# First cross-attention on one Trainium2 core: every second score row passed over by VectorE in one 2048-column instruction, score banks in a cycle of four units

## The reference, cut to what matters

```python
q, k, v = _fq_sym(q, -1), _fq_sym(k, -1), _fq_sym(v, 2)   # round(x / s) * s, s = max|x| / 127
attn = jnp.einsum('bhqd,bhkd->bhqk', q, k)                 # 16 heads x 2048 queries x 2048 keys
attn = jax.nn.softmax(attn.astype(jnp.float32), axis=-1)
attn = _fq_unsigned(attn, axis=-1)                         # round(p / s) * s, s = max(p) / 255 of the row
out = jnp.einsum('bhqk,bhkd->bhqd', attn, v)
x = _layernorm(x + out @ Wp + bp)
```

## Time and profile before

| | |
|---|---|
| median of 3 runs | 2745.82 us (2744.62 to 2748.7) |
| the profiled execution | 2758.03 us, of which the trace's span is 2756.2 us |
| TensorE, matmuls busy | 2339.5 us (85%) |
| VectorE busy | 1871.3 us (68%) |
| ScalarE busy | 1590.1 us (58%) |
| GpSimd busy | 716.9 us (26%) |
| attention stage, first to last instruction of L1753 | 920.3 to 1589.0 us |

### The profile page before, as it was taken

How to read it: one execution, slowest core, us unless ns; L and a number is a source line. 1 busy time by engine, 2 the same in 40 slices (tenths; PEclk the granted TensorE clock), 3 DMA queues, 4 the chain that set the end, 5 groups by cost and what they waited for, 6 DMA issues and landing times. The chain is left out here.

```text
span 2756.2 us, 50448 instructions
## 1 busy us (share of the span) xinstructions
PE 2339.5 (85%) x16399; PEld 1534.9 (56%) x16545; DVE 1871.3 (68%) x4371; ACT 1590.1 (58%) x3099; POOL 716.9 (26%) x897
## 2 busy tenths in 40 slices
PE   6999999999987567777777779889997986899994
PEld 3676766767664334444444445545555664467773
DVE  5877778777774789999999912246665775234444
ACT  3656666566653579989999921056664654123332
POOL 1121121211211112222222200011111267436664
PEclk9999999999998799989889989989999998899997
DMA  5000000000001399999999930040000012446666
GB/s 198 1 1 0 0 0 0 0 0 0 0 0 46 65 207 183 176 185 180 179 184 183 186 77 1 0 148 1 1 1 7 13 64 78 143 86 110 108 108 143
DMA packets 539447, 211.18 MB, mean 77 GB/s; under 512 B 475002, under 2 KB 533878, under 8 KB 538230
## 3 DMA queue, kind: packets, MB, share of 16 engines
q1 hardware_dynamic: 518246, 180.54, 32.6%
q0 software_dynamic: 20592, 27.98, 5.9%
q10 hardware_dynamic: 416, 0.16, 0.0%
HBM read 54.27 MB, written 36.90 MB: 33 GB/s over the span
## 5 line engine op out<-in xcount | busy, mean ns | idle before, releaser
L1753 DVE TENSOR_SCALAR_CACHE_REDUCE x_row<-x_p_s,x_nsq 128x1024 f32<-128x1024 f32 x512 | 621.7, 1270 | 22.4 <-PE x_p_s L1528 22.3
L1632 ACT ACTIVATE x_ints<-x_row,x_nb 128x2048 uint16<-128x2048 f32 x256 | 511.5, 1999 | 46.4 <-DMA x_turned<-x_ints 27.6
L1528 PE MATMUL x_p_s<-x_kT,x_qz 128*128 128x512 bf16 x929 | 299.6, 412 | 145.0 <-DVE x_row L1753 137.6
L363 POOL TENSOR_TENSOR a_rstd<-a_ssq,neghalf 128x16 f32<-128x16 f32 x32 | 126.0, 3936 | 524.7 <-DVE a_ssq L874 524.7
L1528 PEld LDWEIGHTS x_p_s<-x_kT,x_qz 128*128 128x128 bf16 x1024 | 73.6, 101 | 266.7 <-DVE x_row L1753 238.7
L1656 POOL TENSOR_SCALAR x_nb<-x_low,x_hmin 128x1 f32<-128x1 f32 x256 | 75.0, 293 | 519.5 <-DVE x_row L1753 518.2
L3277 POOL DMA_INDIRECT f_acc<-f_yt,f_ids x111 | 171.9, 1548 | 136.3 <-ACT f_yt L3442 109.6
L1562 PEld LDWEIGHTS x_p_o<-x_vi,x_turned 128*128 128x128 f16 x4096 | 143.8, 98 | 87.1 <-DMA x_turned<-x_ints 18.7
L2216 ACT COPY s_eT<-sc_p_e 128x512 f32<-128x512 f32 x192 | 112.3, 585 | 133.7 <-PE sc_p_e L2106 133.6
L1562 PE MATMUL x_p_o<-x_vi,x_turned 128*128 128x16 bf16 x4096 | 143.0, 171 | 16.9 <-DMA x_turned<-x_ints 16.6
L3367 PE MATMUL f_p_g<-f_w,f_rowsT 128*128 x444 | 151.6, 464 | 0.0
(11 more groups left out here) (479 smaller groups left out, 5337.8 us busy)
## 6 DMA issues: line engine op xcount, KB each, us to landing
f_rows<-f_spread SPq DMA_DIRECT2D x111, 136.5 KB, 2.1
f_w<-in_L_ffn_w_dram SPq DMA_DIRECT2D x2, 2816.0 KB
x_turned<-x_ints SPq DMA_TRANSPOSE x224, 4.8
f_sum<-f_acc SPq DMA_DIRECT2D x6, 512.0 KB, 7.2
f_w<-in_L_ffn_w_dram SPq DMA_DIRECT2D x2, 1408.0 KB
f_spread<-f_empty SPq DMA_DIRECT2D x17, 136.5 KB, 2.6
x_res<-in_x_dram SPq DMA_DIRECT2D x2, 1024.0 KB, 6.9
a_wq<-in_L_attn_Wq_dram SPq DMA_DIRECT2D x2, 1024.0 KB, 11.0
```

Of the source, the lines that this page charges most:

```text
L363: pool.tensor_tensor(rstd[:, hs], ssq[:, hs], core.neghalf[:, 0:NH], ALU.pow).then_inc(root_h.sem, 1)
L1528: mm = pe.matmul(p_s[n % SLOTS][:, c * BANK:(c + 1) * BANK], qz[b % 2][:, par, a, :], kT[:, a, at:at + BANK], start=True, stop=True)
L1632: act.activation(ints[k][:, :], rows[k][:, :, :].rearrange("p s n -> p (s n)"), ACT.Exp, bias=nb[:, k:k + 1], scale=-1.0, accum_out=esum[: ...
L1753: dve.tensor_scalar(rows[k][:, half, :], p_s[n % SLOTS][:, :], nsq[:, b % 2, h:h + 1], HIGHEST, ALU.mult, ALU.min, accum_out=(low if half ...
```

## The change

The units with even `j` are passed over by one VectorE instruction of 2048 columns, which waits for all four matmuls and frees four banks at once. The odd units keep their two halves. The three slots become one tensor of six banks, and which pair of banks a half gets follows a cycle of four units (`PAIRS_OF`): an even unit gets two neighbouring pairs, (0, 1) or (1, 2), an odd one the pairs that come free around it. TensorE's order changes with it: at an odd step it makes the second half of that unit and both halves of the next one, at an even step only the first half of the next unit, and that behind `values`. `shift` uses `hmin` twice for an even unit, and `divided` moves from `j` = 4 to `j` = 5 on VectorE.

```diff
--- before.py
+++ after.py
@@ -1420,7 +1420,7 @@
         rden, o_raw, o, oT = sb("rden", [P, XH]), sb("o_raw", [P, H]), sb("o", [P, H]), sb("oT", [P, KT, P])
         y, stats, mv, ln_r = sb("y", [P, H]), sb("stats", [P, 6]), sb("mv", [P, 2]), sb("ln_r", [P, 1])
 
-        p_s = [ps(f"p_s{i}", [P, HALF]) for i in range(SLOTS)]
+        p_s = ps("p_s", [P, SLOTS * HALF])
         p_o, p_w = ps("p_o", [P, BANK]), ps("p_w", [P, BANK])
 
 
@@ -1437,6 +1437,20 @@
         v_turn, v_steps, v_scaled, v_up = (sem(n) for n in ("v_turn", "v_steps", "v_scaled", "v_up"))
         t_made, t_read = sem("t_made"), sem("t_read")
         block = ctx.enter_context(nc.Block())
+
+        PAIRS_OF = ((0, 1), (2, 0), (1, 2), (0, 2))
+        freed, last_user = {}, {}
+        for u in range(UNITS):
+            for half in range(2):
+                pair = PAIRS_OF[u % 4][half]
+                freed[u, half] = last_user.get(pair, 0)
+            for half in range(2):
+                last_user[PAIRS_OF[u % 4][half]] = 2 * u + (half + 1 if u % 2 else 2)
+
+        def scores_at(u, half, n=1):
+
+            at = PAIRS_OF[u % 4][half] * HALF
+            return p_s[:, at:at + n * HALF]
 
         def by_array(u):
 
@@ -1515,19 +1529,25 @@
                     mm = pe.matmul(p_w[:, 0:H], oT[:, t, :], wp[:, t, :], start=False, stop=(t == KT - 1))
                 mm.then_inc(y_made, 1)
 
-            def scores(u):
+            def scores(u, half):
                 b, j = divmod(u, PER_TILE)
                 a, par = divmod(j, 2)
                 if not j:
                     pe.wait_ge(qz_up, b + 1)
-                for half in range(2):
-                    n = 2 * u + half
-                    after(pe, half_up, n - SLOTS + 1)
-                    for c in range(2):
-                        at = half * HALF + c * BANK
-                        mm = pe.matmul(p_s[n % SLOTS][:, c * BANK:(c + 1) * BANK], qz[b % 2][:, par, a, :], kT[:, a, at:at + BANK],
-                                       start=True, stop=True)
-                    mm.then_inc(s_made, 1)
+                after(pe, half_up, freed[u, half])
+                for c in range(2):
+                    at = half * HALF + c * BANK
+                    mm = pe.matmul(scores_at(u, half)[:, c * BANK:(c + 1) * BANK], qz[b % 2][:, par, a, :], kT[:, a, at:at + BANK],
+                                   start=True, stop=True)
+                mm.then_inc(s_made, 1)
+
+            def scores_ahead(u):
+
+                if u % 2:
+                    scores(u, 1)
+                    if u + 1 < UNITS:
+                        for half in ((0, 1) if u % 4 == 1 else (1, 0)):
+                            scores(u + 1, half)
 
             def turn_ints(j, half):
                 def run(b):
@@ -1575,15 +1595,19 @@
                     mm = pe.matmul(p_o[:, t * P:(t + 1) * P], svcol[:, t, :], core.ident[:, :], start=True, stop=True)
                 mm.then_inc(v_turn, 1)
 
+            for half in range(2):
+                scores(0, half)
             for u in range(UNITS + PER_TILE):
                 if u < UNITS:
-                    scores(u)
+                    scores_ahead(u)
                 if not u:
                     turn_largest()
                 if u == 1:
                     turn_scales()
                 if 0 <= u - LATE < UNITS:
                     values(u - LATE)
+                if u < UNITS and not u % 2:
+                    scores(u + 1, 0)
                 jobs(u, {1: [(turn_x, 1)], 3: [(project_q, 1)], 5: [(turn_ints(2, 0), 0)], 6: [(turn_ints(2, 1), 0)],
                          7: [(turn_ints(4, 0), 0)], 8: [(turn_ints(4, 1), 0)],
                          10: [(turn_reps, 1)], 13: [(turn_o, -1)], 15: [(project_o, -1)]})
@@ -1653,7 +1677,8 @@
             def shift(u):
                 k = u % ROWS_KEPT
                 pool.wait_ge(half_up, 2 * u + 2)
-                pool.tensor_scalar(nb[:, k:k + 1], low[:, k:k + 1], hmin[:, k:k + 1], LOG_AMAX, ALU.min, ALU.add).then_inc(nb_up, 1)
+                other = low if u % 2 else hmin
+                pool.tensor_scalar(nb[:, k:k + 1], other[:, k:k + 1], hmin[:, k:k + 1], LOG_AMAX, ALU.min, ALU.add).then_inc(nb_up, 1)
 
             def heads(ap):
                 return ap.rearrange("p (h d) -> p h d", d=XD)
@@ -1744,13 +1769,19 @@
             def pass_over(u, half):
                 b, h = divmod(u, PER_TILE)
                 k = u % ROWS_KEPT
-                n = 2 * u + half
-                dve.wait_ge(s_made, n + 1)
+                whole = not u % 2
+                if whole and half:
+                    return
+                dve.wait_ge(s_made, 2 * u + (2 if whole else half + 1))
                 if not half:
                     after(dve, e_up, u - ROWS_KEPT + 1)
                     if not h:
                         dve.wait_ge(nsq_up, b + 1)
-                dve.tensor_scalar(rows[k][:, half, :], p_s[n % SLOTS][:, :], nsq[:, b % 2, h:h + 1], HIGHEST, ALU.mult, ALU.min,
+                if whole:
+                    dve.tensor_scalar(rows[k][:, :, :].rearrange("p s n -> p (s n)"), scores_at(u, 0, 2), nsq[:, b % 2, h:h + 1], HIGHEST,
+                                      ALU.mult, ALU.min, accum_out=hmin[:, k:k + 1]).then_inc(half_up, 2)
+                    return
+                dve.tensor_scalar(rows[k][:, half, :], scores_at(u, half), nsq[:, b % 2, h:h + 1], HIGHEST, ALU.mult, ALU.min,
                                   accum_out=(low if half else hmin)[:, k:k + 1]).then_inc(half_up, 1)
 
             def quantize_values():
@@ -1788,7 +1819,7 @@
                 jobs(u, {4: [(denominators, -1)], 5: [(inverse, 1)], 1: [(statistics, -2)]})
                 if u < UNITS:
                     pass_over(u, 1)
-                jobs(u, {3: [(largest, 1)], 4: [(divided, -1)], 1: [(moments, -2)]})
+                jobs(u, {3: [(largest, 1)], 5: [(divided, -1)], 1: [(moments, -2)]})
                 if u == ROWS_KEPT - 1:
                     quantize_values()
```

## The result

The changed kernel takes 2762.4 us (median of 3 runs, 2760.7 to 2763.8) against 2745.8: a measured ratio of 1.0044, 95% interval 1.0025 to 1.0064 (the two medians as they stand give 1.0060, inside it). It is slower, by 7 to 18 us, where 7.4 us less were forecast. The profiled execution took 2763.8 us.

The account below looks back on a forecast made before the run. VectorE was taken to bound the stage, with ScalarE close behind. The terms -17.4 + 3.5 + 5.5 + 1 = -7.4 us took 2745.8 to 2738.4 us; the forecast's own range was 2732 to 2743, the full range 2727 to 2757.

Parts of the forecast that it names:

- Costed at nothing: `project_q` and `turn_x` come one unit (2.4 us) later at ScalarE's queue; claimed hidden by four `rows` buffers, at no cost.
- at T + 2.3 against 2.4, no wait at the full clock: `divided`, moved behind the pass its `values` waits for; T is the end of the tile's last pass; no wait claimed.
- Term 1: VectorE's joined passes: 2.274 us for a whole pass, 0.136 saved on each of 128, -17.4 us (0 to 18.9 saved).
- Term 2: Bank fills freed only one half pass (1.20 us) ahead come late at the half clock: +3.5 us (0 to 7).
- Term 3: `project_o` before the next fill: at the half clock VectorE waits 1.6 us instead of 0.82, +5.5 us (0 to +18).
- Start and end: The first pass waits for four matmuls instead of two, and ScalarE is further behind at the end: +1 us.
- The long wait near 1000 us: VectorE's single 10.4 us wait for scores, where the next stage's weights are loaded; taken as unchanged.
- ScalarE becomes the bound: ScalarE's two waits are not absorbed, a tile costs 41.6 us instead of 40.82: +12.5, slower, 2758 us; chance 0.12.
- The clock gives way: TensorE at the half clock for twice the share, PEclk below about 0.85: +11, slower, 2757 us; chance 0.11.
- TensorE held by ScalarE: `turn_ints` waits in TensorE's queue for ScalarE's copy; about 8 us come through: 2746 us, no change; chance 0.20.
- Cover holds: The half clock falls elsewhere than on `project_o`, waits for scores stay as they are: 2729 us; chance 0.20.

Follow-up runs that it names:

- largest_late: The changed kernel with VectorE's `largest` and GpSimd's `scales` one unit later (`j` = 4 instead of 3): ratio 1.0008 to the kernel before.
- query_early: The changed kernel with `project_q` on TensorE one step earlier (`j` = 2 instead of 3): ratio 1.0001 to the kernel before, 1.0013 when measured again.
- before_query_late: The kernel before, without joined passes, with `project_q` on TensorE one step later (`j` = 4 instead of 3): ratio 1.0063 to the kernel before.
- split: The changed kernel with even units passed over by two 1024-column instructions again, banks and TensorE's order as changed: ratio 1.0122 to the kernel before.
- after_again: The changed kernel itself, measured once more beside the kernel before on another chip: ratio 1.0038 to the kernel before.

## Why the prediction was wrong

It gave 2738.4 us with a range to 2757.0; 2762.4 lies outside, on the slower side, which had a chance of 0.23.

- **The failed step: "Costed at nothing".** It saw that `project_q` and `turn_x` come one unit later, "and ScalarE's queue stands at both", and hid that behind the four `rows` buffers. ScalarE's queue was not the one that mattered. The copy `query_up` has another reader: `largest` on VectorE, at step 3 of the same tile. Measured: +20.2 us (21.4 against 1.2), in all 15 tiles. With it at zero or nearly so (`largest_late`, `query_early`) the kernel is level with before; with it alone (`before_query_late`) the kernel before loses 0.63%.
- **The same step, `divided`:** "at T + 2.3 against 2.4, no wait at the full clock". It waited 0.74 us right behind the timeline above (at 1242.10), 5.6 us up to 1605 us, where the kernel before has 0.5 beside the 7.1 of its last tile. At the full clock the margin held: `divided` did not wait in seven of the 15 tiles, and in all seven the granted clock was 1.00 in the stretch of the fills before it (3.4 to 0.6 us ahead). In seven others it waited 0.73 to 0.76 us, and there that clock was 0.50 (the last, at 0.73, waited 0.40). The prediction priced the half clock for two other places, and put it at nothing here.

```profile
1241.27 0.08 DVE L1784 DVE_READ_ACCUMULATOR x_row<-x_p_s,x_nsq 128x1 f32 x1
1242.10 0.42 DVE L1758 TENSOR_TENSOR x_o_raw<-x_p_o,x_rden 128x256 f32<-128x256 f32 x1 [0.74 <-issue]
```

- **Term 1, -17.4, was right but for 2 us.** A whole pass starts 2.27 to 2.28 us before the next (1236.44 to 1238.71, for one), where 2.274 was worked out. Added up over VectorE's timeline, from start to start without the waits, all passes but the last take 599.1 us against 614.6, so 15.5 are saved; the half passes take 1.209 each instead of 1.203. `split` confirms the sign.
- **Term 2, +3.5, in kind and size.** The whole pass of unit 14 waits 0.4 us in 12 of the tiles, 4.7 us in all; it lies within 0 to 7. In the 3 us before these waits the granted clock was 0.52 to 0.63, so they are the fills at the half clock that the term describes.
- **Term 3, +5.5, did not occur.** The kernel before has seven waits of 0.82 us behind `project_o` between 1040 and 1590 us (the prediction counted six); the change has none there. `project_o`'s weight loads, 1055 to 1600 us, last 190 ns from the shortest to the longest, which is the full clock, where the kernel before has a median of 264 over the stage. The chain holds at the full clock, as worked out. That I carried the share of half clock over, and placed it on this product, was the mistake: it stood at unit 14 and in front of `divided`. The rows of the two products (ns: shortest, median, longest), after:

```profile
L1529 PEld LDWEIGHTS x_p_w<-x_wp,x_oT x56: 190/190/190, 1062.0 to 1595.5; 128*128 128x128 f32 x56
```

and before:

```profile
L1515 PEld LDWEIGHTS x_p_w<-x_wp,x_oT x64: 190/264/337, 1017.5 to 1603.3; 128*128 128x128 f32 x64
```

- **Start and end, +1:** the tail alone took 2.9 us more, 1.6 of it by ScalarE's end. The long wait near 1000 us, taken as unchanged, went from 10.4 to 6.7.
- **The sum as measured,** between the starts of the first pass and the last: -15.5 by the passes, +20.2 at `largest`, +5.1 at `divided`, and 3.2 us less at the passes themselves (16.8 against 20.0) give +6.6, where 6.8 was measured. Then 2.9 for the tail.
- **Rivals.** *ScalarE becomes the bound* gave the time nearest to what was measured (2758), for the wrong reason: no pass waited for an exponential in the change. *The clock gives way* did not occur: 0.93 against 0.91. *TensorE held by ScalarE* was hidden in the change itself behind the wait of `largest`, and came through as soon as that was taken away (`query_early`, 9.2 us where it had said 8). *Cover holds* was right of `project_o` only.

What would have caught it: for every instruction that moves later on TensorE, follow its result through the copy to every reader, not only to the engine that copies. The earlier trace rows showed that ScalarE waited 15.5 us for `project_q` already, so any microsecond more went straight on. The prediction used that row for ScalarE's own time, and did not look up the row of `largest`, which already waited for `query_up` six times.

## What to carry to other kernels

A product that is moved behind a longer group of work must be followed to the last engine that reads it, above all when that is the bounding one: one step of `project_q` costs the kernel before 17 us, as much as 128 joined passes were to give. When an instruction is joined to save its fixed part, its inputs are wanted all at once and its buffers come free all at once, so the short jobs of the feeding engine need their places chosen anew, in front of or behind each fill; the best order found here keeps at most a third of the saving. And a kernel before with the same moves is the twin to compare with: without it, the moved product's own gain would have been put down to the joined pass.

## What the runs showed of the hardware

The granted clock of the stage rose with the change (0.91 to 0.93, and 0.93 again in `after_again`), although TensorE's waits were gathered into fewer and longer ones (220 of 0.71 us between 1010 and 1590, against 239 of 0.58). With the query early it went the other way: 0.94 and 0.95 in the two twins without joined passes, 0.89 to 0.92 in the eight versions with them. But the kernel before with the query late has 0.94 too, so of the four profiles of the kernel before and its moved queries, only its own is at 0.91. The Trainium skill (TensorE: Matmul & The Clock Gate, "A second HAM failure mode: psum-queue depth-cycling") says that short idle times between groups of matmuls, from cycling through PSUM banks, make the clock oscillate. That is not borne out by the change and its before, and agrees in direction with the pairs with the query early; no run here separates its mechanism from the place of the waits.

A pass of VectorE over 2048 fp32 columns in PSUM, in one instruction with an accumulator, takes 2.27 us from start to start, over 1024 columns 1.205: two of the latter take 0.14 us more than one of the former.
